# Four shared PSUM banks for scores and transposed probabilities, one per row group, and an earlier second self-attention score call

## The reference

```python
x = x + xattn(layernorm(x), ctx, ctx, mask)  # 16 heads of 32; 512 keys a batch
x = x + attn(layernorm(x))                   # 16 heads of 32; the 64 tokens of the batch
x = x + ffn(layernorm(x))                    # relu, weights quantised to -1, 0, 1; 2048 hidden

def xattn(Q, K, V, mask):
    q, k, v = split(Q @ W_Q.T), split(K @ W_K.T), split(V @ W_V.T)
    e = where(mask, -inf, q @ k.T / sqrt(32))   # the mask is one row of 512 keys, for all
    return merge(softmax(e) @ v) @ W_O.T
```

## Time and profile before

| | |
|---|---|
| median of three executions | 1761.74 us |
| the profiled execution | 1761.58 us |
| its span, first to last instruction | 1759.8 us |
| TensorE busy, share of the span | 96% |
| VectorE, ScalarE, GpSimd busy | 59%, 40%, 12% |
| TensorE's granted clock, mean | 0.988 |
| cross stage, self stage, feed-forward stage | to about 772, 1277, 1760 us |

### The profile page before, as it was taken

One profiled execution on the slowest core, in us unless ns is written; L12 is line 12 of the kernel. 1 busy time (PEld: TensorE's weight loads), 2 busy tenths in 40 slices (PEclk: granted clock), 3 DMA queues, 4 the chain that ended last, 5 costly groups with the idle time before them and its releaser, 6 DMA issues.

```text
span 1759.8 us, 38870 instructions
## 1 busy us (share of the span) xinstructions
PE 1690.6 (96%) x16268; PEld 1418.7 (81%) x16268; DVE 1031.1 (59%) x1492; ACT 702.0 (40%) x1689; POOL 212.6 (12%) x300
## 2 busy tenths in 40 slices
PE   6899999999999999989999999999599999999999
PEld 4688878887888888878898989888478888888887
DVE  3655555555555555667677777778554445445533
ACT  2555555555666555656332222222122222222221
POOL 1000000000000000032021212120222022202200
PEclk9999999999999999999999999999799999999999
DMA  5011111111111111341100101010101001101000
GB/s 216 13 61 61 61 62 61 61 61 56 57 59 61 62 61 61 141 157 66 40 34 30 42 24 48 24 48 13 73 31 48 33 16 48 48 4 43 24 25 24
DMA packets 48668, 95.00 MB, mean 54 GB/s; under 512 B 5792, under 2 KB 14112, under 8 KB 47264
## 3 DMA queue, kind: packets, MB, share of 16 engines
q1 hardware_dynamic: 48544, 93.16, 15.3%
HBM read 67.97 MB, written 25.17 MB: 53 GB/s over the span
## 4 chain that ended last, share of the span: by engine, by line
PE 89%; DVE 6%; issue 2%; ACT 2%; DMA 1%; SPq 0%; DVEq 0%; ACTq 0%
PE project L331 49%; PE project L1669 13%; PE scores L677 4%; PE scores L1683 3%; PE scores L1685 3%; PE probs_t_psum L1685 3%; PE probs_t_psum L1683 3%; PE probs_t_psum L686 3%; PE attended_t L703 2%; PE probs_t_psum L1328 2%; PE scores L483 1%; PE attended_t L1347 1%; DVE ff_weight_scratch L1548 1%; PE attended_t L1230 1%; DVE w_ternary L1551 1%
## 5 line engine op out<-in xcount | busy, mean ns | idle before, releaser
L1669 PE MATMUL project<-ff_xt,w_ternary 128*128 128x512 f32 x1024 | 255.9, 392 | 1.7 <-DVE ff_xt L1242 1.7
L1669 PEld LDWEIGHTS project<-ff_xt,w_ternary 128*128 128x128 f32 x1024 | 190.1, 188 | 40.3 <-issue 1.9
L1718 ACT ACTIVATE hidden<-project,b_sb 128x512 f32<-128x512 f32 x128 | 88.3, 690 | 325.3 <-PE project L1669 324.1
L1743 DVE CAST hidden_hi<-hidden 128x512 fp32r<-128x512 f32 x128 | 56.7, 443 | 229.9 <-ACT hidden L1718 228.9
L879 ACT ACTIVATE cross_scores_probs<-cross_scores_probs,exp_bias,logit_scale 128x128 f32<-128x128 f32 x256 | 122.7, 482 | 96.9 <-DVE exp_bias L1025 96.9
L331 PE MATMUL project<-self_xt_hi,self_w_hi 128*128 128x256 f32 x512 | 149.3, 292 | 3.2 <-DVE self_xt_lo L494 2.3
L331 PE MATMUL project<-self_xt_lo,self_w_hi 128*128 128x256 f32 x512 | 145.9, 285 | 0.0
L331 PE MATMUL project<-self_xt_hi,self_w_lo 128*128 128x256 f32 x512 | 145.9, 285 | 0.0
L879 ACT ACTIVATE cross_probs<-cross_scores,exp_bias,logit_scale 128x128 f32<-128x128 f32 x256 | 122.8, 483 | 0.4 <-DVE exp_bias L1025 0.4
L331 PE MATMUL project<-ctx_hi,cross_w_hi 128*128 128x512 f32 x256 | 106.7, 417 | 15.2 <-DVE ctx_lo L1044 15.2
L331 PE MATMUL project<-cross_w_hi,ctx_hi 128*128 128x512 f32 x256 | 108.7, 425 | 0.0
(11 more groups left out here) (154 smaller groups left out, 3819.4 us busy)
## 6 DMA issues: line engine op xcount, KB each, us to landing
ctx_raw<-in_ctx SPq DMA_DIRECT2D x64, 256.0 KB, 3.9
cross_xt_raw<-in_x_t SPq DMA_DIRECT2D x64, 128.0 KB, 2.1
cross_x<-in_x SPq DMA_DIRECT2D x32, 256.0 KB, 2.9
x<-cross_x SPq DMA_DIRECT2D x32, 256.0 KB, 2.0
self_x<-x SPq DMA_DIRECT2D x32, 256.0 KB, 2.8
ff_w_raw<-in_w SPq DMA_DIRECT2D x2, 4096.0 KB, 14.2
x<-self_residual SPq DMA_DIRECT2D x32, 256.0 KB, 2.0
ff_x<-x SPq DMA_DIRECT2D x32, 256.0 KB, 3.5
```

The lines of the kernel that those rows point to most:

```text
L1669: last = nc.tensor.matmul(PJ[m % 2][:], w1_q[:, c, cols], x_t[parity(v)][:, c, :], start=(c == 0 and x_t is fxt_hi), stop=(c == DC - 1 and ...
L1718: nc.scalar.activation(h_raw[:, m % 2, :], PJ[m % 2][:], ACT.Relu, bias=b1_sb[:, m:m + 1]).then_inc(h_relu, 1)
L1743: nc.vector.tensor_copy(h_hi[:, m % 4, :], h_raw[:, m % 2, :]).then_inc(h_hi_ready, 1)
```

## The change

Scores and transposed probabilities now share one PSUM tensor `SPT` of four banks: columns 0 to 255 of each bank are scores (`S`), columns 256 to 511 transposed probabilities (`PT`). `place(head)` gives row group r (head % 4) bank r for itself, and the column half is the parity of the chunk (head // 4). Since two engines may not be in one bank at a time, waits are added: `scores` waits for the copies of earlier transposes, `transposes` for VectorE to have read the scores that were issued before it. The access patterns of VectorE and ScalarE follow the new layout. In the order of work, these things move: the last cross unit does S3 in the middle of the V projection and A3 ahead of the first self scores; in the self stage S1 comes between Q0 and Q1, T0 after K0 and A0 after K1; ScalarE takes K0 out ahead of `probs_t_out` 0; VectorE does `divide(u, 1)` ahead of `a_hi` and `a_lo`.

```diff
+def place(head):
+    chunk, group = divmod(head, 4)
+    return 2 * group + chunk // 2, chunk % 2
...
-        S = outer.enter_context(nc.psum_tensor("scores", [P, 1024], F32))
-        PT = outer.enter_context(nc.psum_tensor("probs_t_psum", [P, 1024], F32))
+        SPT = outer.enter_context(nc.psum_tensor("scores_and_probs_t", [P, 4, 512], F32))
+        S, PT = SPT[:, :, 0:256], SPT[:, :, 256:512]
...
         def self_score_products(half, t):
-            for c in range(DC):
-                for b in range(2):
-                    for r in range(4):
-                        rows, at = slice(DK * r, DK * r + DK), SEQ * (r % 2)
-                        col = SLOT[2 * c + r // 2] * P + b * SEQ
-                        last = nc.tensor.matmul(S[at:at + SEQ, col:col + SEQ],
+            for c_low, b, c_high, r in itertools.product(range(0, DC, 2), range(2), range(2),
+                                                         range(4)):
+                c, rows = c_low + c_high, slice(DK * r, DK * r + DK)
+                slot, side = place(4 * c + r)
+                col = P * (slot % 2) + SEQ * b
+                last = nc.tensor.matmul(S[SEQ * side:SEQ * side + SEQ, slot // 2, col:col + SEQ],
...
             def scores(u, q):
                 wait(e, C.s_free, total(u, 4, q))
+
+                wait(e, C.pt_ready, total(u, 4, max(0, q - 1)))
                 n = K.kt * P
                 for c in (range(DC) if K.kt == 1 else (q,)):
                     for r in range(4):
-                        rows, half = slice(DK * r, DK * r + DK), SEQ * (r % 2)
-                        slot = K.slot(2 * c + r // 2)
+                        rows = slice(DK * r, DK * r + DK)
+                        slot, half = K.place(4 * c + r)
...
             def transposes(u, q):
                 wait(e, C.pt_ready, total(u, 4, q))
+
+                wait(e, C.s_free, total(u, 4, min(4, q + 2)))
                 wait(e, C.p_norm, total(u, 4, q + 1))
...
+                attend(u, 3)
                 self_score_products(0, 0).then_inc(G.s_full, 1)
-                attend(u, 3)
...
-                    scores(u, 3)
-                    self_v(u, 0)
+                    self_v(u, 0, lambda: scores(u, 3))
...
             def scores(u, t):
 
                 wait(e, G.s_shifted, total(u, NT, t))
+
+                wait(e, G.pt_ready, total(u, NT))
                 self_score_products(parity(u), t).then_inc(G.s_full, 1)
 
             def transposes(u, t):
                 wait(e, G.pt_ready, total(u, NT, t))
+
+                wait(e, G.s_shifted, total(u, NT, NT))
                 wait(e, G.p_norm, total(u, NT, t + 1))
...
+                scores(u, 1)
                 if more:
                     qk_proj(u, "Q1", 0, kind)
-                scores(u, 1)
+                    qk_proj(u, "K0", 1, kind)
                 transposes(u, 0)
                 if more:
-                    qk_proj(u, "K0", 1, kind, lambda: attend_waits(u, 0))
+                    qk_proj(u, "K1", 1, kind, lambda: attend_waits(u, 0))
                 else:
                     attend_waits(u, 0)
                 attend(u, 0)
                 if more:
-                    qk_proj(u, "K1", 1, kind)
                     v_proj(u, 0, kind)
...
+                if more:
+                    qk_out(u, v, "K0", kind)
                 probs_t_out(u, 0)
                 exponentials(u, 1)
-                if more:
-                    qk_out(u, v, "K0", kind)
...
+                divide(u, 1)
                 a_hi(u)
                 a_lo(u, 0)
-                divide(u, 1)
```

More of the change, by code:

```diff
@@ L474, in self_v_products @@
                 (sxt_hi[:, c, rows], sxt_lo[:, c, rows], sw_hi[:, 2, c, :], sw_lo[:, 2, c, :])
[L475 removed]
+                for c in range(DC)], before_last, half_way)
         def self_score_products(half, t):
[L478 to L486 removed]
+            for c_low, b, c_high, r in itertools.product(range(0, DC, 2), range(2), range(2),
[4 more added lines that the diff above has]
+                last = nc.tensor.matmul(S[SEQ * side:SEQ * side + SEQ, slot // 2, col:col + SEQ],
+                                        sq_t[rows, half, c, 2 * t + b, :],
+                                        sk_t[rows, half, c, 2 * t + b, :],
+                                        start=True, stop=True)
             return last
@@ L533, in __init__ @@
                 self.batch = (lambda q: q) if kt == 1 else (lambda q: 0)
-                self.slot = ((lambda pair: (pair % 2) * 4 + pair // 2) if kt == 1 else
-                             (lambda pair: pair % 2))
+                self.place = place if kt == 1 else (lambda head: ((head % 4) // 2, head % 2))
                 self.x = x.rearrange("(u t p) d -> u t p d", t=self.nt, p=self.tp)
@@ L672, in scores @@
                     for r in range(4):
-                        rows, half = slice(DK * r, DK * r + DK), SEQ * (r % 2)
-                        slot = K.slot(2 * c + r // 2)
+                        rows = slice(DK * r, DK * r + DK)
+                        slot, half = K.place(4 * c + r)
                         keys = (ck_t[parity(u)][rows, c, q, :] if K.kt == 1 else
                                 ck_t[parity(u)][rows, c, :, :].rearrange("p j k -> p (j k)"))
-                        last = nc.tensor.matmul(S[half:half + SEQ, slot * n:(slot + 1) * n],
-                                                cq_t[rows, c, K.batch(q), :], keys,
-                                                start=True, stop=True)
+                        for k in range(0, n, 256):
+                            at = slot * n + k
+                            width = min(n, 256)
+                            last = nc.tensor.matmul(
+                                S[SEQ * half:SEQ * half + SEQ, at // 256, at % 256:at % 256 + width],
+                                cq_t[rows, c, K.batch(q), :], keys[:, k:k + width],
+                                start=True, stop=True)
                 last.then_inc(C.s_full, 1)
@@ L701, in attend @@
                     for k in range(K.kt):
-                        at = (K.slot(head // 2) * K.kt + k) * P + SEQ * (head % 2)
+                        slot, half = K.place(head)
+                        at = (slot * K.kt + k) * P + SEQ * half
                         last = nc.tensor.matmul(
@@ L1014, in maxima @@
                 wait(e, C.s_full, total(u, 4, q + 1))
+                if K.kt == 1:
+                    split = lambda a: a.rearrange("p r (j k) -> p r j k", k=n_keys)
+                    bias = mask_bias[:, KEYS - n_keys:KEYS].unsqueeze(1).unsqueeze(1) \
+                        .to_broadcast([P, 4, 2, n_keys])
+                else:
+                    split = lambda a: a.rearrange("p (g h) k -> p g h k", h=2)
+                    bias = mask_bias[:].rearrange("p (h k) -> p h k", h=2).unsqueeze(1) \
+                        .to_broadcast([P, 2, 2, 256])
                 nc.vector.tensor_tensor(
-                    rows(c_s[q % 2]), rows(S),
-                    mask_bias[:, KEYS - n_keys:KEYS].unsqueeze(1).to_broadcast([P, groups, n_keys]),
+                    split(c_s[q % 2].rearrange("p (r n) -> p r n", r=4)), split(S), bias,
                     ALU.add).then_inc(C.s_free, 1)
@@ L1345, in attend @@
                         col = (t * DC + head // 4) * SEQ
-                        at = SLOT[head // 2] * P + SEQ * (head % 2)
+                        slot, half = place(head)
+                        at = slot * P + SEQ * half
                         last = nc.tensor.matmul(
@@ L1877, in _ @@
             e.wait_ge(mask_step, 2)
-            nc.tensor.matmul(S[0:1, 0:2], counts[:, 1:2], ones[:, 0:2], start=True, stop=True) \
+            nc.tensor.matmul(SPT[0:1, 0, 0:2], counts[:, 1:2], ones[:, 0:2], start=True, stop=True) \
                 .then_inc(mask_counted, 1)
```

33 lines of the change are left out of this document (18 added, 15 removed).

## The result

The changed kernel takes 1809.64 us (median of 4, 1805.89 to 1812.07) against 1760.53 for the kernel before (1758.59 to 1763.2): ratio 1.0276, 95% interval 1.0252 to 1.0300. It is slower, as forecast, but by 49 us where 5 to 6 were forecast, and so it lies outside the range. The profiled execution has a span of 1807.0 us, 47.2 more than before, at a mean granted clock of 0.973 in place of 0.988.

The account below looks back on a forecast made before the run. TensorE, busy 96% of the span, was taken to set the pace of both attention stages. 1761.6 - 18.1 (cross) + 21.3 (self) + 2 (clock) = 1767 us, with a range of 1752 to 1784.

Parts of the forecast that it names:

- units 1 to 3 and the clock: Self stage: units 1 to 3 lose 2.1 us each, 6.3 in all; one fall of the clock adds 2.
- unit 0: First unit of the self stage: counted at -3.1 us, between +0.5 and -3.5.
- units 14, 15: Last two units of the self stage: -0.6 us and +0.7 us.
- Part 1: Scores: eight array tiles run at once instead of four, 0.44 us off each cross call; the self gains are lost.
- the rival of four tiles: Scores: four tiles remain the limit, cross scores gain nothing, total 1785 us; chance 0.12.
- Part 2: Cross stage: T0 newly waits for the mask addition of scores 1, losing 0.57 us; stage in all -18.1 us.
- Part 3: Self stage: T0 newly waits for the second maxima, TensorE idles 1.9 us a unit; stage in all +21.3 us.
- Rival (d): Self stage: T0's new wait doesn't bind, only the cross gain is left, 1740 us; chance 0.07.
- (b): Self stage: GpSimd's chain loses 1.0 us in each of ten units, total 1755 us; chance 0.12.
- The clock: Self stage: a fall behind T0's new gap costs 1.6 us; one fall is taken, +2 us.
- rival (c): Self stage: the clock falls in every other unit, total 1776 us; chance 0.17.
- the check by the period: Self units: period 14.4 + 17.2 = 31.6 to 31.7 us against 29.86, so +1.8 a unit.

Follow-up runs that it names:

- e1: Changed kernel with 80 more TensorE instructions in the four-tile cross program, which does not run, so the self loop's code lies further on; 1766.32 us, ratio 1.0030.
- e9: e1's placement and order, but column half r % 2 as in the kernel before, row groups still on separate banks; 1784.24 us, ratio 1.0131.
- e7: e1 with VectorE's second maxima ahead of layer norm (self) and mask addition of scores 1 ahead of the first division (cross); 1732.55 us, ratio 0.9842.
- e4: Changed kernel with 40 more TensorE instructions in the four-tile cross program, which does not run; 1766.1 us.
- e8: Changed kernel with 110 more TensorE instructions in the four-tile cross program, which does not run; 1786.4 us.
- e10: Changed kernel with 20 more TensorE instructions in the four-tile cross program, which does not run; 1800.8 us.
- e2: Kernel before with 175 more TensorE instructions in the four-tile cross program, which does not run; 1789.14 us, ratio 1.0158.
- e5: e1 with each row group's first two chunks on column half 0 and last two on half 1, own bank kept; 1767.95 us.

## Why the prediction was wrong

The direction was right, and it would have been so without the surprise (e1: ratio 1.0030, 1.0019 to 1.0041). Most terms that stand in the sum were close; the cross stage was off by up to 3.5 us. What failed is a term that doesn't stand in it. The comparison, with e1 for the changed kernel with its loop's code kept:

| step | forecast, us | measured, us |
|---|---|---|
| cross call of scores | 1.03 to 0.6 | 1.03 to 0.62 |
| cross unit | -1.17 | -1.06 |
| cross stage | -18.1 | -14.6 in e1, -15.6 after |
| idle time before T0, self | 1.9 | 1.70 to 1.74 in e1 |
| units 4 to 13, each | +1.8 | +1.73 in e1 |
| units 1 to 3 and the clock | +6.3 + 2 | +8.5 in e1 |
| unit 0 | -3.1 | -3.9 in e1 |
| units 14, 15 | -0.6, +0.7 | -0.7, +1.0 in e1 |
| place of the self loop's code | 0, not considered | +43 in time, after against e1 |
| total | 1767 | e1 1766.3, after 1809.6 |

**Part 1** was right, for the reason given: e9 shows the tiles, and the rival of four tiles (1785) is what e9 gives with 1784.2. That the gain of the self scores would be lost was right as well: with the shorter first call the wait for `a_lo` behind it grows from 0.2 to 0.5 us.

**Part 2** was right in mechanism. T0 waits for the mask addition in the middle units, and the wait cost what e7 gives back, 0.47 a unit. The cross stage fell short by 2.5 to 3.5 us. The 14 middle units gave 14.7 us in e1 and 13.8 in the changed kernel, where the returns of the cross loop stop for 1.0 longer in all than before, against 16.4; the first unit gave 0.7 to 0.8 as forecast; the last gave 0.5 in the changed kernel and lost 0.6 in e1, where 0.9 had been costed from single rows. The rest is when the first scores start: 0.6 earlier in the changed kernel, 0.3 later in e1.

**Part 3** was right to 0.1 us a unit in units 4 to 13. That units 1 to 3 and the clock come out at 8.5 against 8.3 is luck in part: the clock fell twice, not once, for 1.7 us each, and less these 3.4 the longer chain costs 5.1 us there, not 6.3. Rival (d), that the wait doesn't bind, fell. So did (b): GpSimd's additions and VectorE's division stay side by side in e1, and the pair takes what it took in the earlier trace rows:

```profile
1061.10 3.51 POOL L458 TENSOR_TENSOR self_residual<-self_x,bo_sb 128x512 f32<-128x512 f32 x2 [26.31 <-DMA x<-self_residual]
```

**The clock.** No gap before T0 of up to 1.81 us was followed by a fall. Of the 16 gaps before T0 between 1.97 and 2.04 us in all traces 11 were followed by one within 1 us; five were not (after at 808.40, e4 at 809.90, e8 at 1008.70, e10 at 1018.54 and 1158.84). In e1 there is one fall behind T0, in unit 1, as forecast:

```profile
809.27:811.30 2.03, 0.00 (x1) 0.03 (x1) 1.89 (x2) 0.87 (x4) 0.00 (x0) 1.00 0.00 0
811.30:815.00 3.70, 3.70 (x20) 3.70 (x21) 0.15 (x1) 2.15 (x3) 0.00 (x0) 0.56 0.00 0
```

There is a second one that nobody forecast, from 832.24 to 835.65, behind gaps of 1.67 and 0.54 us (828.75 to 830.42, 830.80 to 831.35). Every kernel with shared banks has it; the kernel before, with gaps of 1.67 and 0.44 at that point, does not.

In the changed kernel T0's gap in the odd units is 2.00 to 2.02 us, against 1.70 in e1, where the returns don't stop. So rival (c), a fall in every other unit, came true, through a cause that it didn't name (its own terms give 1775, not 1776).

**The step that failed** is the check by the period in part 3: "The period is 14.4 + 17.2 = 31.6 to 31.7". It counts what each engine executes and waits for, and takes for granted that the next instruction is there. As far as it goes it holds: e1 has 31.60. In the changed kernel each of the loop's five returns stops TensorE for 4.0 to 4.7 us while code is loaded, and a pair of units takes 71.7 us in place of 63.2: 8.5 us more with the falls of the clock, some 43 in all, for a term that stood at nothing. The profile of before could have told: its cross loop, at 1868 instructions, waits for "issue" at its returns and loads instructions, its self loop with 1729 doesn't. A loop so near to the limit made every added instruction, and every one ahead of it, a risk worth a rival of its own.

## What to carry to other kernels

Ahead of a change to a long loop, count the loop's instructions on each engine and look for instruction packets inside it; where there are none and the loop is near the limit (about 7 blocks of 256 here), even code that never runs can cost 1.6% (e2), and the same edit costs 0.3% or 2.8% by its placement alone (e1, after). A stop marked "issue" right behind a loop's return, and once more within the next instructions, is the sign. Where buffers are shared to gain something, look first whether the engine that must free them does so early: here one moved line on VectorE turned the loss of the shared banks (1766) into a gain (1740).

## What the runs showed of the hardware

- A TensorE loop of 1729 or 1735 instructions runs for passes on end without one instruction packet, or loads some 9 packets of 16 KB a pass, by where it lies. A return then stops TensorE for 1.0 to 1.6 us and again for 2.4 to 3.4 us (after, e2, e10), or once for 1.8 to 2.9 us (e8). Behind the double stops TensorE worked at 0.50 of the clock for 3.1 to 6.4 us; of e8's five single stops only those of 1.93 and 2.90 us were followed at once by a fall.
- Gaps of 1.97 to 2.04 us before T0 were followed by a fall of the clock in 11 of 16 cases; gaps of 1.67 and 0.54 us with 0.4 us of work between them were followed by one too (e1), and one of 3.16 us by none (e7, at 1192.01).
- Score products on two column halves of each row group take 0.62 us a call (e1), and 0.65 when 16 matmuls of the program stand between the halves (e5), against 1.03 with each row group on one half (e9): the halves run at once.
- Separate banks alone bring the scores nothing (e9).
